# A gated cross-attention block with a mixture of experts on one core: weight quarters spread over more slots, one broadcast of the inverse sums, low halves on VectorE

## The reference

```python
x = x + jnp.tanh(g_xattn[0]) * xattn(_layernorm(x), ctx_2048, Wq, bq, Wk, bk, Wv, bv, Wo, bo)
x = x + jnp.tanh(g_ffn[0]) * ffn(_layernorm(x), gate_w, w1, w2, w3)

# xattn, x and c are [8, 256, 512]
q = jnp.einsum('oc,bct->bot', Wq, x) + bq[None, :, None]      # k, v the same way, from c
scores = jnp.einsum('bhkt,bhks->bhts', q, k) * 0.25   # SCALE = 1/sqrt(16)
p = jax.nn.softmax(scores, axis=-1)
out = jnp.einsum('bhts,bhks->bhkt', p, v)
return jnp.einsum('oc,bct->bot', Wo, out.reshape(B, H * K, T)) + bo[None, :, None]

# ffn, x is [2048, 512]
probs = jax.nn.softmax(x @ gate_w.T, axis=-1)
top_w, top_i = jax.lax.top_k(probs, 2); top_w = top_w / jnp.sum(top_w, axis=-1, keepdims=True)
for e in range(12):
    h = jax.nn.silu(x @ w1[e].T) * (x @ w3[e].T)
    out = out + h @ w2[e].T * cw[:, e:e + 1]
```

## Time and profile before

| | us |
|---|---|
| median of 3 runs | 817.38 (808.57 to 820.51) |
| the profiled execution | 816.6 |
| its span | 814.9 |
| slots 1 to 9 and the end of slot 0 | 45 to 508 |
| tiles of the experts | 542 to 815 |

### The profile page before, as it was taken

The page is one execution under the profiler, slowest core; times in us unless marked ns, Lnnn a source line. Parts: engine busy times, 40 slices in busy tenths (PEclk is TensorE's granted clock), DMA queues, the critical chain, the costliest instruction groups (busy, mean ns, idle before and its releaser), DMA issues.

```text
span 814.9 us, 14231 instructions
## 1 busy us (share of the span) xinstructions
PE 663.1 (81%) x4335; PEld 303.2 (37%) x4336; DVE 430.0 (53%) x761; ACT 325.1 (40%) x391; POOL 239.7 (29%) x184
## 2 busy tenths in 40 slices
PE   5878976977979879879876825059999999999993
PEld 3712222312222223232221113046666666666661
DVE  5536667585794785665646743753333333333330
ACT  0047855745646556546555610002222222222221
POOL 4032223222331331322111102233354433454422
PEclk8879989998997989879888865569999999999998
DMA  8447877768787887857767537524677787664533
GB/s 249 139 129 241 258 247 247 220 224 277 199 276 200 254 267 215 265 163 200 244 208 207 182 106 259 205 81 92 169 185 212 230 222 205 182 116 91 84 47 39
DMA packets 68470, 155.56 MB, mean 191 GB/s; under 512 B 9733, under 2 KB 15366, under 8 KB 66886
## 3 DMA queue, kind: packets, MB, share of 16 engines
q1 hardware_dynamic: 36368, 76.56, 29.8%
q10 hardware_dynamic: 22422, 55.87, 21.0%
q0 software_dynamic: 9632, 22.55, 14.6%
HBM read 92.04 MB, written 58.46 MB: 185 GB/s over the span
## 4 chain that ended last, share of the span: by engine, by line
PE 49%; DVE 15%; DMA 12%; issue 9%; SPq 8%; POOL 2%; ACT 2%; ACTq 2%; DVEq 0%; POOLq 0%
PE S L1393 15%; PE O L1414 9%; PE O L1253 7%; DMA ocz<-inverse_sums 5%; PE S L1214 5%; SPq L470 4%; DMA out<-yo,slot_out 3%; SPq L477 3%; DVE wp L825 3%; PE MC L1288 3%; PE MA L1288 2%; PE S L1380 2%; ACT prob L724 2%; PE MC L1308 2%; DVE wp L823 2%
## 5 line engine op out<-in xcount | busy, mean ns | idle before, releaser
L724 ACT ACTIVATE prob<-S 128x1024 f32<-128x1024 f32 x256 | 253.2, 1025 | 207.8 <-PE S L1214 144.0
L1253 PE MATMUL O<-prob,V 128*32 128x512 f32 x1024 | 156.0, 685 | 0.1
L1393 PE MATMUL S<-W,xT 128*128 x1032 | 149.9, 303 | 1.2 <-DVE xT L1158 1.2
L1214 PE MATMUL S<-Q,K 48*128 48x512 f16 x512 | 107.9, 428 | 52.2 <-ACT prob L724 46.0
L1393 PEld LDWEIGHTS S<-W,xT 128*128 128x128 f16 x1032 | 100.2, 99 | 39.0 <-issue 1.4
L1214 PEld LDWEIGHTS S<-Q,K 48*128 48x128 f16 x512 | 24.4, 94 | 216.9 <-ACT prob L724 149.7
L652 POOL DMA_INDIRECT out<-yo,slot_out x43 | 69.0, 1604 | 119.8 <-ACT yo L769 71.7
L1414 PE MATMUL O<-W,hT 128*128 (+1 forms) x344 | 90.3, 381 | 1.0 <-DVE hT L1178 1.0
L1166 DVE SCALAR_TENSOR_TENSOR hh<-S,act 128x320 f32<-128x320 f32 x43 | 21.1, 492 | 126.9 <-PE S L1393 124.2
L825 DVE SCALAR_TENSOR_TENSOR wp<-wf,wp 128x1024 f16<-128x1024 f32 x48 | 82.4, 1716 | 1.7
L628 POOL DMA_INDIRECT xg<-tokens_normed,slot_tok x43 | 42.6, 990 | 44.7 <-PE S L1380 32.5
(11 more groups left out here) (152 smaller groups left out, 670.7 us busy)
## 6 DMA issues: line engine op xcount, KB each, us to landing
wf<-wall ACTq DMA_DIRECT2D x48, 512.0 KB, 6.7
weight_parts<-wp ACTq DMA_DIRECT2D x48, 512.0 KB, 4.7
W<-weight_parts SPq DMA_DIRECT2D x10, 2048.0 KB, 9.7
K<-k_parts SPq DMA_DIRECT2D x8, 1024.0 KB, 6.7
Q<-q_parts SPq DMA_DIRECT2D x8, 1024.0 KB, 6.7
k_parts<-ks SPq DMA_DIRECT2D x24, 256.0 KB
q_parts<-qs SPq DMA_DIRECT2D x24, 256.0 KB
ctx<-ctx_in SPq DMA_DIRECT2D x8, 512.0 KB, 6.0
```

Of the source, the lines that this page charges most:

```text
L724: act.activation(prob[:, u % RING, :], S[u % 2][:, :], ACT.Exp, scale=SCALE).then_inc(g.exp, 1)
L1214: last = pe.matmul(S[u % 2][:, s * T:(s + 1) * T], K[par][r0:r0 + rows_, 2 * g4 + n, st * P:(st + 1) * P], Q[par][r0:r0 + rows_, 2 * g4 + ...
L1253: last = pe.matmul(O[g4 % 2][2 * DK * j:2 * DK * (j + 1), :], V[par][:, st, head(g4, j), :], prob[:, u % RING, (j % 2) * T:(j % 2 + 1) * T ...
L1393: last = pe.matmul(ps, xT[par][:, xp * TT + k, :], W[:, bass.ds(off + (w * WCOL + (2 * k + n) * F), F)], start=(k == 0 and (xp, w) == (0, 0)),
```

## The change

- `quarters` spreads the 48 quarters as 4 (slot 0, all at step 15), 8 (slot 1), 4 in each of slots 2 to 7 (steps 2, 6, 9, 12), 8 (slot 8), 2 (slot 9, both at step 7), and 2 between the first two tiles of the experts. There are four buffers `wf`. SP issues the stores, at fixed places of its own program; ACT only waits for the split, three steps later, and issues the next load.
- The values of a slot stay in `osum`: four transfers of 16 partitions write half of them over the sum rows, after the inverse has been taken. The inverse sums come back by one transfer over 128 partitions. Context and x of the next batch are loaded after the K writes instead of first.
- PE issues both score groups of the next step before the extra product. o0 and o1 stand at steps 8 and 9, t0, t1 and lg at 13 to 15; LN_AT, XN2_AT and CS_AT are one later.
- DVE makes the low halves of the context, of x and of the attention's result; POOL keeps those of K, Q and the normed tokens. `xn2` shares the buffer of `xn`.

```diff
     PIECES = 1
     EB = 4
-    WFS = 3
+    WFS = 4
...
-    z_dram = nc.dram_tensor("inverse_sums", [GH, GROUPS, T], F32).ap()
+    z_dram = nc.dram_tensor("inverse_sums", [GH, 2, CT * T], F32).ap()
...
-        oc, zc = ocz[:, 0], ocz[:, 1]
+        zc = ocz[:, 1]
 
         w4 = ocz[:, :, :, :].rearrange("p a b t -> p (a b t)").rearrange("p (n k c) -> p n k c", n=4, k=CT)
         zl = sb("zl", [P, ZW], F32, att)
         zr = sb("zr", [P, ZW], F32, att)
         on = kf
-        xn2 = sb("xn2", [P, CT, T], F32, att)
+        xn2 = xn
...
-        EXTRA = {0: "k0", 1: "k1", 2: "q0", 3: "q1", 4: "v0", 5: "v1", 6: "v2", 7: "o0", 8: "o1a", 9: "o1b",
-                 10: "v3", 12: "t0", 13: "t1", 14: "lg"}
-        ON_AT, LN_AT, XN_AT, XN2_AT, CS_AT, SPLIT_AT = 5, 6, 8, 10, 11, 3
-        OZ = 16 * 4 * GH
+        EXTRA = {0: "k0", 1: "k1", 2: "q0", 3: "q1", 4: "v0", 5: "v1", 6: "v2", 8: "o0", 9: "o1",
+                 10: "v3", 13: "t0", 14: "t1", 15: "lg"}
+        ON_AT, LN_AT, XN_AT, XN2_AT, CS_AT, SPLIT_AT = 5, 7, 8, 11, 12, 3
+        OZ = 16 * (GH + 1)
...
         def quarters(t):
 
-            if t.i is None and t.add in (0, B + 1):
-                return []
-            if t.i is None and t.add == 1:
-                steps, first = (4, 7, 10, 13), At(None, 0, 0)
+            if t.i is None and t.add == 0:
+                steps, first = (15, 15, 15, 15), At(None, 0, 0)
+            elif t.i is None and t.add == 1:
+                steps, first = (1, 3, 5, 7, 9, 11, 13, 14), At(None, 0, 4)
             elif t.i is None and t.add == B:
-                steps, first = (0, 2, 4, 6, 8, 10, 12, 13), At(None, 0, QUARTERS - 8)
+                steps, first = (0, 2, 4, 6, 8, 10, 12, 13), At(None, 0, QUARTERS - 12)
+            elif t.i is None and t.add == B + 1:
+                steps, first = (7, 7), At(None, 0, QUARTERS - 4)
             else:
-                steps = (0, 2, 5, 8, 10, 13)
-                first = At(t.i, 12, 4 + 6 * (t.add - 2)) if t.i is not None else At(None, 0, 4 + 6 * (t.add - 2))
+                steps, first = (2, 6, 9, 12), At(t.i, 4 * t.mul, 4 * t.add + 4)
             return [(v, first.before(-n)) for n, v in enumerate(steps)]
...
+            def store_quarter(q):
+
+                c = q.add % 4
+                wait(sp, s_wlo, q, 1, 1, s_bog)
+                sp.dma_start(w_dram[bass.ds(over(q, 4).value(), 1), :, :, c * WQ:(c + 1) * WQ]
+                             .rearrange("e p h n -> p (e h) n"), wp[q.add % 2][:, :, :]).then_inc(s_wst[q.add % 2], 16)
...
+                    splits = [] if guard else quarters(t)
+
+                    def weights(v0, v1):
+                        for v, q in splits:
+                            if v0 <= v < v1:
+                                store_quarter(q)
+
+                    def over_sums(j):
+
+                        r0 = 2 * DK * j
+                        sp.dma_start(osum[par][r0 + DK:r0 + 2 * DK, 0:CT, :], osum[par][r0:r0 + DK, CT:2 * CT, :])\
+                            .then_inc(g.oz, 16)
+
+                    def write(dram, parts, part, rows_, st):
+                        for r in rows_:
+                            sp.dma_start(dram[:, r], parts[:, part].rearrange("p m t -> p (m t)")).then_inc(st, 16)
+
+                    def read(stack, dram):
+                        sp.dma_start(stack[par][:, :, :].rearrange("p (g m) t -> p g (m t)", m=CT),
+                                     dram.rearrange("(g s) r c n -> (s r c) g n", s=2)).then_inc(g.qk, 16)
+
+                    if c:
+                        bc = t.before(2)
+
+                        wait(sp, g.os, bc, GROUPS, GROUPS, s_bog)
+                        wait(sp, g.on, bc, 1, 1)
+                        sp.dma_start(zl[:, :], osum[par][DK::2 * DK, :, :]).then_inc(g.zl, 16)
+                        wait(sp, g.rz, bc, 1, 1)
+                        sp.dma_start(z_dram.rearrange("j h n -> (j h n)").rearrange("(p n) -> p n", p=P), zr[:, :])\
+                            .then_inc(g.zst, 16)
+                        for j in range(GH):
+                            over_sums(j)
+                    if a:
+
+                        wait(sp, g.qk, t, KQ_READS, 0, s_bog)
+                        wait(sp, g.kh, t, 1, 1)
+                        write(k_dram, ks, 0, (0, 1), g.kst)
+                    if c:
+
+                        wait(sp, g.zst, bc, 16, 16)
+                        sp.dma_start(zc.rearrange("p m t -> p (m t)"),
+                                     z_dram.rearrange("j h n -> (j h) n").unsqueeze(1).to_broadcast([2 * GH, DK, CT * T]))\
+                            .then_inc(g.oz, 16)
+                    if a:
+                        wait(sp, g.kl, t, 1, 1)
+                        write(k_dram, ks, 1, (2,), g.kst)
...
+                        weights(3, 10)
+                    else:
+                        weights(0, 9)
...
+                    weights(10 if a else 9, VS)
...
-                sp.wait_ge(s_wst[n], 16 * 2 * NE)
+                sp.wait_ge(s_wst[n], 16 * (2 * NE - 1))
...
+                if e == NE - 1:
+                    for n in range(2):
+                        sp.wait_ge(s_wst[n], 16 * 2 * NE)
...
-                    if c:
-                        lo_part(bc, os_, on, g.oh, g.ol)
                     if p:
                         inverse_spread(nxt, mv, veps, rstd, g.mv, g.veps, g.rstd)
-                        lo_part(nxt, xs, xn, g.xh, g.xl)
                     if c:
                         inverse_spread(bc, mv2, veps2, rstd2, g.mv2, g.veps2, g.rstd2)
                         wait(pool, g.x2h, bc, 1, 1)
                         pool.tensor_tensor(xs2[:, 1], xn2[:, :, :], xs2[:, 0], ALU.subtract).then_inc(g.x2l, 1)
-                    if p:
-                        lo_part(nxt, cs, ctx_sb, g.ch, g.cl)
...
+            def load_behind(q):
+
                 if q.i is not None or q.add + WFS < QUARTERS:
+                    wait(act, s_wlo, q, 1, 1, s_bias)
                     load_quarter(q.before(-WFS))
 
             def attention(act, g, guard):
                 def slot(act, t, par, a, b_, c, p):
                     splits = [] if guard else quarters(t)
                     if not b_:
+                        if a and not guard:
+                            for n in range(WFS):
+                                load_quarter(At(None, 0, n))
+                        for _, q in splits:
+                            load_behind(q)
                         return
-                    if not guard and t.i is None and t.add == 1:
-                        for n in range(WFS):
-                            load_quarter(At(None, 0, n))
                     b = t.before(1)
                     for u in range(2 * VS):
                         wait(act, g.full, b, 2 * VS, u + 1)
@@ -723,8 +743,8 @@
                         wait(act, g.pv, b, VS, u // 2 - RING // 2 + 1)
                         act.activation(prob[:, u % RING, :], S[u % 2][:, :], ACT.Exp, scale=SCALE).then_inc(g.exp, 1)
                         for v, q in splits:
-                            if u == 2 * min(v + 2, VS - 1) + 1:
-                                store_quarter(q)
+                            if u == 2 * min(v + 3, VS - 1) + 1:
+                                load_behind(q)
...
+            def last_store(q):
+                act.wait_ge(s_wlo, q + 1)
+                act.dma_start(w_dram[q // 4, :, :, q % 4 * WQ:(q % 4 + 1) * WQ], wp[q % 2][:, :, :])\
+                    .then_inc(s_wst[q % 2], 16)
...
+                if j.i is None and 1 <= j.add <= 2:
+
+                    last_store(QUARTERS - 3 + j.add)
...
+                def x_normed(b, shared=False):
                     wait(dve, g.rstd, b, 1, 1)
 
                     wait(dve, g.xl, b, 1)
+                    if shared:
+                        wait(dve, g.xnst, b, 16, -32)
...
-                            dve.tensor_tensor(on[:, :, :], oc[:, :, :], zc[:, :, :], ALU.mult).then_inc(g.on, 1)
+                            dve.tensor_tensor(on[:, :, :], osum[par][:, 0:CT, :], zc[:, :, :], ALU.mult)\
+                                .then_inc(g.on, 1)
                             wait(dve, g.on, bc, 1, 2)
                             dve.tensor_copy(os_[:, 0], on[:, :, :]).then_inc(g.oh, 1)
+                            low(bc, os_, on, g.oh, g.ol)
...
-                            x_normed(nxt)
+                            x_normed(nxt, c)
+                            low(nxt, xs, xn, g.xh, g.xl)
                         if c and v == XN2_AT:
                             wait(dve, g.rstd2, bc, 1, 1)
 
                             wait(dve, g.xnst, bc, 16, 16)
+                            if p:
+                                wait(dve, g.xl, nxt, 1, 1)
...
                         if p and v == CS_AT:
                             ctx_high(nxt)
+                            low(nxt, cs, ctx_sb, g.ch, g.cl)
...
```

(10 more changed lines are left out.)

49 lines of the change are left out of this document (6 added, 43 removed).

## The result

The changed kernel takes 844.16 us (median of 4 runs, 838.97 to 846.73), the kernel before 814.65 in the same comparison (4 runs, 808.57 to 820.51): ratio 1.036, 95% interval 1.026 to 1.046. Slower, where 783 us and a gain were forecast; the range, 760 to 806, does not hold it. The profiled execution after spans 844.4 us against 814.9 before.

A forecast was written before the change was run, and what follows sets the result against it. No engine was full; waits and DVE-POOL collisions cost each steady slot 13.7 us. From 816.6: -44 (slots 2 to 7), +16 (slots 0 and 1), -6.6 (slot 8), +0.5, +0.5 gave 783 us, range 760 to 806.

The forecast's parts named there:

- the store of step 3 lands at 91: Slot 1: this store waits behind the read of Q, so the split of step 7 makes DVE stand 8 us.
- a store behind the tokens' store, about 4: Slot 8: the split of step 13 waits about 4 us for a store queued behind the tokens' store.
- with the 6.0 us of a 512 KB load and its issue it lands at 217.8: Steady slot: broadcast of inverse sums, out at 211.1, lands then; DVE waits 1.4 us, PE stalls 1.6 at V.
- Clock dips behind these two stalls: 0.8: Slots 2 to 7: lower clock after PE's stalls at V and t1 costs 0.8 us a slot.
- The need of a slot, 42.1 us, and 48.5 with its terms: Slots 2 to 7: 42.1 us if nobody is late, plus ACT 1.0, V 1.6, t1 3.0, clock 0.8.
- t1, 3.0 us: Slot's end: DVE empties t0 at about 244, PE wants the bank for t1 at 241; stall 3.0 us.
- The 7 us of cover for the store of step 6: Slots 2 to 7: the store lands at 234, the split of step 12 needs its buffer at 241.
- Slots 0 and 1, +16, and slot 8, 42.6: Late exponentials and waits for stores cost the first two slots 16 us; slot 8 takes 42.6 instead of 49.2.
- The head, 10.5 us: Slot 1: ACT's loads wait for slot 0's splits, first exponential at 56.5, shifting the slot by 10.5 us.
- The end, +1.0: Slot 9 +0.5 us, and the last two splits beside the tiles of the experts +0.5.
- slower: Rival: SP's queue closes into a ring (read of Q, store of step 6, split of step 12, t1); 840 us, chance 0.06.
- Slots stay at 55: Rival: waits move from ACT to other places, only slots 0 and 1 change; 822 us, chance 0.07.

The follow-up runs named there:

- F5: E3 with DVE's product with the inverse sums, its cast and low half at step 6 instead of 5: 794.40 us, ratio 0.977.
- E3: The changed kernel with ACT instead of SP issuing each store of a split quarter, right before the load that follows it: 817.62 us, ratio 0.998.
- F2: E3 with the broadcast of inverse sums cut to its first quarter (128 KB), most of the context divided by stale numbers: 782.95 us, ratio 0.959.
- K3: G1 with the loads of the next context and x issued behind the first two Q writes instead of ahead: 808.24 us, ratio 0.987.
- K2: F5 with the old numbers and steps of splits (none in slot 0, six in each of slots 2 to 7): 801.47 us, ratio 0.982.
- F3: E3 with the three low halves (context, normed tokens, next context) given back to POOL: 811.41 us, ratio 0.994.
- G4: F5 with the three low halves on POOL, as before the change: 803.22 us, ratio 0.975.
- G1: F5 with no splits in slot 0, eight in slot 1, five in slot 6, seven in slot 7: 797.53 us, ratio 0.970.
- K1: The changed kernel, stores still on SP, with the product with the inverse sums at step 6 instead of 5: 845.22 us, ratio 1.024.
- G3: The kernel before the change with the product with the inverse sums at step 6 instead of 5: 802.30 us, ratio 0.971.
- K4: G1 with the broadcast issued ahead of the two writes of K's high half instead of behind them: 782.14 us, ratio 0.955.

## Why the prediction was wrong

The forecast for the profiled execution was 783 us, and it took 846.2. Stage by stage the miss is 13.2 us in slots 0 and 1 (+29.2 for +16), 34.4 in slots 2 to 7 (-9.6 for -44), 13.1 in slot 8 (+6.5 for -6.6) and 2.3 in the rest. Of the 34.4 us the profile of F5, in which both of the following faults are mended, gives back 30.5 (54.2 to 49.1 us a slot). Two steps failed above all: the price of the stores on SP, and the landing of the broadcast together with what stands behind the wait for it.

- **The stores on SP** ("the store of step 3 lands at 91", in slot 8 "a store behind the tokens' store, about 4") failed: they were priced with the 4.7 us of the earlier trace rows, which were issued from ACT's own queue. On SP they stand behind the read of Q, the broadcast and the tokens' store. Slot 1's wait was seen, at 8 us; it measured 11.7. In slot 8 the wait behind the tokens' store was put at 4 us and took 5.8; the one of 10.4 behind the broadcast was not seen at all. A landing of 6 us alone does little harm: in F5 the stores on ACT take 6.2 us (4.2 in E3) and splits wait 10.5 us for them in all, not 38.2. Worth, by E3, all of the loss, 1.036 to 0.998.
- **"with the 6.0 us of a 512 KB load and its issue it lands at 217.8"** failed: 8.6 to 9.8 us from issue to product in slots 2 to 7, 6.9 in slot 9 where little is beside it. I took the row of a plain load; F2 shows that the bytes count, K3 and K2 (12.5 to 13.4 us) that the neighbours do, and slot 9 that the transfer alone leaves half of the DMA engines' time unused, for a cause that stays open. By the estimate from the Trainium skill (SBUF — State Buffer, "The DMA setup-cost knee") it would have been 3.2 us; the measurement decides against it, in slot 9 too. The forecast's stall of PE at V, 1.6 us, became 3.7. V1 need not stand behind this wait: F5 moves it ahead and takes 3.5 us a slot off E3.
- **"Clock dips behind these two stalls: 0.8"** was too small: the same matmuls take 44.2 us at a granted 0.88 and 41.6 at 0.96, 2.6 us in one slot, 3.4 in the mean of six. A stall costs itself and the stretch at the low level behind it, seen best in the logits, 3.59 us. The sum also took the logits at 1.6 us because it read their 1.96 us in the earlier trace rows as time at a lower clock; the granted clock there (250.76 to 252.72) was 1.00.
- **The need of a slot, 42.1 us, and 48.5 with its terms.** F5, with both faults mended, has slots of 49.1 in the mean, but part of this agreement is luck: slot 7, which prepares nothing, takes 42.5 and slots 2 and 3 take 54.5 and 53.2; slots 4 to 6 take 47.7 to 48.6. DVE's work was right (34.2 us, 35.2 forecast). Four splits for six, with their new steps, is what brings the gain (K2, 5.7 us a slot). The Trainium skill's rule on the blocking of DVE and GpSimd (SBUF — State Buffer, "Who interferes with whom") agrees with the rows: a split's second instruction takes 1263 ns in the mean with the low halves on DVE and 1563 with them on POOL. But F3 and G4 show no worth that can be measured, either way.
- **t1, 3.0 us:** 3.7 at the longest, 2.7 in the mean: right.
- **The 7 us of cover for the store of step 6** were enough: no split of slots 2 to 7 waited for a store, although the read of Q left 28.6 to 33.6 us into these slots and not 26.
- **Slots 0 and 1, +16, and slot 8, 42.6:** E3 comes near both (+17.8 and 41.1), but that is luck: these numbers hold waits for stores of 8 and 4 us, and E3 has 2.5 us of them in slot 1 and 1.6 in slot 8. What was too low is the eight splits for four in slot 1: with none in slot 0 and the stores on ACT (G1) slot 2 still starts 6.0 us later than before. The head, 10.5 us, was right (11.7 between F5 and G1).
- **The end, +1.0:** +3.3. The two waits for inverse sums and splits in slot 9 are in it; what else was not tried.
- **The rivals:** the "slower" one, given 0.06, was the closest in time (840), by luck: its ring was not what lengthened the changed kernel, whose steady slots had no wait for a store. It showed itself in the profile of K1. "Slots stay at 55" (0.07) had the slots right for another reason.

How much of the difference between F5, G1, G3 and K4 is real stays open: F5, G1 and K4 ran on different chips, and neighbouring intervals overlap.

## What to carry to other kernels

A landing time belongs to the queue and the company in which it was measured: before moving a transfer to another queue, list what will stand ahead of it there and what waits for it, at the irregular ends of the loop too. When an engine must wait for a late transfer, first look at what stands behind that wait in its order; moving the wait one step was worth 2.9% in the old kernel, as much as the whole change with two repairs. And two faults may hide each other: mended alone (K1), the second showed no gain that four executions could tell from none.

## What was not expected of the hardware

- A 512 KB broadcast from eight 4 KB rows took 6.5 to 7.1 us from issue to product in slot 9, beside little else, 8.6 to 9.8 in the changed kernel's slots 2 to 7 and 12.5 to 13.4 in K2; 128 KB took 2.8 and 5.8. Alone it kept the DMA engines busy for a share of 0.50 to 0.52. Cut in eight it took no less, with 5.0 to 5.8 us of issuing in most slots.
- A 256 KB write issued behind a 1 MB read of the same queue (253.11 in K1) let the read that waits for it go only 13 us later.
